# The router's steps at other places of the iteration, and exponentials first in each score unit

## What is computed

```python
h = _layernorm(x) * (1 + ca) + sa
A1 = where(causal, Q1 @ K1.T * scaling, -inf)        # per head; A2 alike
attn = softmax(A1, -1) - lam * softmax(A2, -1)
O = attn @ V;  O = O / rms(O) * rms_scale * (1 - LAMBDA_INIT)
x = x + ga * (O @ W_o.T)
h = _layernorm(x) * (1 + cb) + sb
logits = h @ router_w.T + router_b                   # 8 experts
topv, topi = top_k(logits, 2);  gates = softmax(topv)
x = x + gb * sum_e gate_e * (silu(h @ gate_w_e.T) * (h @ up_w_e.T)) @ down_w_e.T
```

## Time and profile before

| what | value |
|---|---|
| time, median of 3 runs | 1676.66 us (1676.61 to 1682.93) |
| profiled execution, device time | 1678.91 us |
| its span, first to last instruction | 1677.1 us |
| what lies around the span | 1.8 us |
| busy: PE / DVE / ACT / POOL | 1340.8 / 1228.7 / 859.4 / 857.3 us |
| mean granted TensorE clock | 0.903 of full |

### The profile page before, as it was taken

The page is one execution under the profiler, slowest core; times in us unless marked ns, Lnnn a source line. Parts: engine busy times, 40 slices in busy tenths (PEclk is TensorE's granted clock), DMA queues, the critical chain, the costliest instruction groups (busy, mean ns, idle before and its releaser), DMA issues. The chain is left out here.

```text
span 1677.1 us, 44178 instructions
## 1 busy us (share of the span) xinstructions
PE 1340.8 (80%) x14048; PEld 940.4 (56%) x14049; DVE 1228.7 (73%) x3090; ACT 859.4 (51%) x1918; POOL 857.3 (51%) x1283
## 2 busy tenths in 40 slices
PE   1578888888888888888888888885199999999960
PEld 0345555555555555555555555553178888888850
DVE  3467887888888888888888888876756666666647
ACT  1156667666766676667666766664123333333320
POOL 0135566666666666666666666665323333333334
PEclk9999989998999899989998999896589999999985
DMA  5453444344434443444344434410111111111129
GB/s 203 99 111 76 112 109 101 86 111 109 105 85 108 112 105 84 111 111 105 83 111 111 106 83 108 105 39 17 43 44 44 44 44 46 43 44 45 44 76 296
DMA packets 182624, 151.73 MB, mean 90 GB/s; under 512 B 29555, under 2 KB 165369, under 8 KB 182068
## 3 DMA queue, kind: packets, MB, share of 16 engines
q1 hardware_dynamic: 165124, 122.11, 30.2%
q0 software_dynamic: 8448, 16.93, 3.3%
q10 hardware_dynamic: 8880, 10.49, 1.8%
HBM read 88.26 MB, written 60.51 MB: 89 GB/s over the span
## 5 line engine op out<-in xcount | busy, mean ns | idle before, releaser
L1190 DVE TENSOR_REDUCE mx<-p_max 128x2 f32<-128x512 f32 (+1 forms) x768 | 504.9, 685 | 198.3 <-PE p_max L816 188.9
L1009 ACT ACTIVATE probs<-p_exp 128x512 f32<-128x512 f32 x768 | 440.4, 601 | 239.7 <-PE p_exp L837 150.9
L1430 POOL TENSOR_SCALAR_AFFINE_SELECT probs<-probs 128x256 f32<-128x256 f32 (+1 forms) x768 | 366.3, 486 | 344.6 <-ACT probs L1009 333.3
L866 PE MATMUL p_out<-probs,v 128*32 128x256 f32 (+1 forms) x4096 | 253.3, 371 | 42.1 <-ACT ot L1000 35.7
L659 POOL DMA_INDIRECT pair_out<-on,v x136 | 133.7, 983 | 282.4 <-ACT on L569 274.6
L808 PE MATMUL p_max<-kt,qt 50*128 50x256 bf16 x1024 | 199.3, 293 | 35.6 <-ACT probs L1009 19.0
L866 PEld LDWEIGHTS p_out<-probs,v 128*32 128x32 f32 x4096 | 124.0, 119 | 145.2 <-POOL probs L1430 67.9
L837 PE MATMUL p_exp<-qt,kt 52*128 52x256 bf16 x1024 | 205.2, 289 | 0.0
L816 PE MATMUL p_max<-tri,ids 64*128 64x128 bf16 (+1 forms) x768 | 188.7, 253 | 0.0
L633 DVE TENSOR_TENSOR ot<-ot,p_max 128x512 f32<-128x512 f32 x136 | 93.5, 688 | 123.6 <-PE p_max L520 105.0
L816 PE MATMUL p_max<-tri,idb 64*128 64x128 bf16 (+1 forms) x768 | 172.3, 252 | 0.0
(11 more groups left out here) (174 smaller groups left out, 2750.5 us busy)
## 6 DMA issues: line engine op xcount, KB each, us to landing
qt<-q_parts SPq DMA_DIRECT2D x128, 192.0 KB
q_parts<-part_h SPq DMA_DIRECT2D x96, 128.0 KB, 1.9
kt<-k_parts SPq DMA_DIRECT2D x128, 96.0 KB
v<-rows_sorted SPq DMA_DIRECT2D x136, 65.0 KB, 1.8
q_parts<-part_m SPq DMA_DIRECT2D x64, 128.0 KB, 1.9
kt<-k_parts SPq DMA_DIRECT2D x128, 64.0 KB
qt<-pair_out SPq DMA_DIRECT2D x32, 256.0 KB, 5.0
mods<-mod_rows SPq DMA_DIRECT2D x32, 192.0 KB
```

The costliest lines, as they stand in the source:

```text
L866: m = nc.tensor.matmul(p_out[32 * j:32 * j + 32, pair, SEQ - n:SEQ], v[:, b.par, tile, 2 * g + head, :], src, start=(tile == 0), stop=(til ...
L1009: nc.scalar.activation(probs[:, quad % 2, k, :], p_exp[:, n % 3, :], ACT.Exp, scale=SCALE).then_inc(exp_done.sem, 1)
L1190: V.reduce_max(mx[:, w, tile, t, heads[0]:heads[-1] + 1], p_max[:, bank, :].rearrange("p (h k) -> p h k", h=len(heads)), AX.X, negate=True ...
L1430: G.affine_select(out=blocks, in_=blocks, compare_op=ALU.is_ge, fill=zero, base=0, pattern=[[0, count], [1, P]], channel_multiplier=-1).th ...
```

## The change

Router steps move, and the order inside a score unit is turned round. PE: logits from s=7 to s=5; the two `outputs_to_rows` of half 1 from s=5 and 6 (banks 1 and 0) to s=5 and 7 (banks 0 and 1); ranks from s=10 to s=11. DVE: `lg` from s=8 to s=6, the top eight from s=9 to s=7, the second `normalise` of half 1 from s=7 to s=8, after `minus_max`; statistics of bW from s=8 and 9 to s=10; positions from s=11 to s=12. ACT: `gexp` from s=10 to s=9. POOL: `o` from s=8 to s=9, `osq` from s=9 to s=10, scatters from one in each of s=12 to 15 to one in s=13, two in s=14 and one in s=15. The work is the same, and so is its amount.

```diff
-        MISC0 = [(ht_ready, 1, 2), (r_ready, 1, 2), (r_ready, 2, 2), (on2_ready, 4, -1),
+        MISC0 = [(ht_ready, 1, 2), (r_ready, 1, 2), (r_ready, 2, 2), (on2_ready, 3, -1),
                  (v_ready, 1, 1), (on2_ready, 1, 0)]
         MISC1 = [(nmt_ready, 2, 0), (ont_ready, 1, -2), (attn_scaled, 1, -2), (h2t_ready, 1, -3),
-                 (on2_ready, 3, -1), (route, 1, -3), (nmt_ready, 1, 1), (route, ROUTE_CARRY, -3),
+                 (route, 1, -3), (on2_ready, 4, -1), (nmt_ready, 1, 1), (route, ROUTE_CARRY, -3),
                  (on2_ready, 2, 0)]
...
-                for _ in itertools.zip_longest(max_unit(bm, n), exp_unit(be, n)):
+                for _ in itertools.zip_longest(exp_unit(be, n), max_unit(bm, n)):
...
                     if s == 5 and active(bC):
-                        outputs_to_rows(i, bC, 1, 0, 1, 4)
-                    if s == 6 and active(bC):
-                        outputs_to_rows(i, bC, 1, 1, 0, 3)
+                        outputs_to_rows(i, bC, 1, 0, 0, 3)
...
-                    if s == 7 and active(bR):
-                        mix_free(pe, i, 1, 5)
+                    if s == 5 and active(bR):
+                        mix_free(pe, i, 1, 4)
                         wait(pe, h2t_ready, bR)
...
                         m.then_inc(lg_ps.sem, 1)
+                    if s == 7 and active(bC):
+                        outputs_to_rows(i, bC, 1, 1, 1, 5)
...
-                    if s == 10 and active(bR):
+                    if s == 11 and active(bR):
 
                         mix_free(pe, i, 1, 7)
                         wait(pe, route, bR, ROUTE_BOTH)
...
-                    if s == 10 and active(bR):
+                    if s == 9 and active(bR):
                         wait(act, route, bR, ROUTE_TOP)
...
                     if s == 6:
+                        if active(bR):
+
+                            wait(dve, route, bR.plus(-1))
+                            wait(dve, lg_ps, bR)
+                            V.tensor_tensor(lg[:], p_mix[:, 1, 0:NT * NE].rearrange("p (t e) -> p t e", t=NT),
+                                            rb[:].unsqueeze(1).to_broadcast([P, NT, NE]), ALU.add).then_inc(route.sem, 1)
                         for k in range(2):
                             if active(bC):
-                                normalise(bC, 1, 0, 1, k)
+                                normalise(bC, 1, 0, 0, k)
...
-                    if s == 7 and active(bC):
-                        for k in range(2):
-                            normalise(bC, 1, 1, 0, k)
+                    if s == 7 and active(bR):
+                        wait(dve, route, bR, 1)
+                        settle(dve)
+                        for tile in range(NT):
+                            V.max(top8[:, tile, :], lg[:, tile, :]).then_inc(route.sem, 1)
                     if s == 8:
                         if active(b1):
                             minus_max(b1, 0, 0)
                             minus_max(b1, 0, 1)
...
+                        if active(bC):
+                            for k in range(2):
+                                normalise(bC, 1, 1, 1, k)
...
+                    if s == 10 and active(bW):
+                        wait(dve, x1_ready, bW)
+                        settle(dve)
+                        statistics(bW, 1, stats2)
+                        for tile in range(NT):
+                            mean_and_variance(bW, 1, stats2, tile)
...
                     if s == 11:
                         inverse_roots(i, [0])
+                    if s == 12:
                         if active(bR):
 
                             wait(dve, rank_ps, bR)
...
-                    if s == 12:
                         hrow = h2[:, bR.par].rearrange("p j t r -> p (j t) r")
...
-                    if s == 8 and active(bC):
+                    if s == 9 and active(bC):
 
                         wait(pool, on2_ready, bC)
...
-                    if s == 9 and active(bC):
+                    if s == 10 and active(bC):
                         wait(pool, o_ready, bC)
...
-                    if s in (12, 13, 14, 15) and active(bR):
-
-                        k = s - 12
+                    for k in {13: (0,), 14: (1, 2), 15: (3,)}.get(s, ()):
+                        if not active(bR):
+                            continue
```

More of the change, by code:

```diff
@@ L1316, in body @@
                     if s == 6:
-                        for k in range(2):
-                            if active(bC):
-                                normalise(bC, 1, 0, 1, k)
-                            if active(bL):
-                                mean_and_variance(bL, 0, stats1, k)
-                    if s == 7 and active(bC):
-                        for k in range(2):
-                            normalise(bC, 1, 1, 0, k)
[L1325 to L1328, removed]
                         if active(bR):
@@ L1334, in body @@
                                             rb[:].unsqueeze(1).to_broadcast([P, NT, NE]), ALU.add).then_inc(route.sem, 1)
[L1335 to L1338, removed]
-                    if s == 9:
[L1340 to L1347, removed]
+                        for k in range(2):
+                            if active(bC):
+                                normalise(bC, 1, 0, 0, k)
+                            if active(bL):
+                                mean_and_variance(bL, 0, stats1, k)
+                    if s == 7 and active(bR):
[3 more added lines that the diff above has]
+                            V.max(top8[:, tile, :], lg[:, tile, :]).then_inc(route.sem, 1)
+                    if s == 8:
+                        if active(b1):
+                            minus_max(b1, 0, 0)
+                            minus_max(b1, 0, 1)
+                        if active(bC):
+                            for k in range(2):
+                                normalise(bC, 1, 1, 1, k)
+                    if s == 9:
                         if active(bR):
```

## The result

The changed kernel takes 1685.82 us (median of 19 runs), the one before, run alongside, 1680.43; the ratio is 1.0039, 95% interval 1.0021 to 1.0058. That is 0.4% slower: clear of noise, within the 0.5% that the prediction calls no change, and opposite to the forecast of 1618 us. Ratios leave out executions in a slower state that shows now and then, so they can differ a little from the quotient of the medians.

A forecast was written before the change was run, and what follows sets the result against it. PE bounds steps 0 to 5, DVE the rest. Per iteration 2.16+2.06-1.5-0.3=2.4 us, taken as 2.1; over 28 iterations 59 us, so 1618 us for the median; likeliest case 1604 to 1642, whole range 1602 to 1688.

The forecast's parts named there:

- its two halves: One iteration: PE bounds steps 0 to 5, busy 8.55 of 9.30 us; DVE bounds the rest, busy 19.59 of 22.20.
- light stretch of PE: From 573.4 to 579.4 us PE is busy only 3.35 of 6.00; right after it the clock stands at half for 6.8.
- the idle time of DVE that goes: DVE's waits of 0.70, 0.93 and 0.43 us for PE go if the clock stays at 2.4 GHz: 2.06, 0.5 left.
- the first term: DVE saves 2.16 us an iteration because `minus_max` no longer meets `o` and `topf` no longer meets `osq`.
- if nothing new collides: Condition on DVE's saving of 2.16 us: the moved POOL operations hold no other DVE operation.
- Rival 2: `o` meets `chosen` or `both` and DVE stands still for nearly 1.28 us; time 1668 to 1695 us; chance 0.22.
- The forecast's upper end: Slow end of the forecast's range, 1642 us, beside a smallest gain of 39 us over the loop.
- The pair of units: Exponentials first delay the second unit's maximum by 0.11 or 0.22 us; exposed at s=3 and s=5, 0.3 an iteration.
- Rival 3: The clock's fall moves to steps 0 to 4, where PE bounds; 36 us slower if in all iterations, 1713; chance 0.08.
- Moved at no cost: `gexp` on ACT, the scatters on POOL and half 1's second `normalise` in step 8 move without adding time.
- The wait for `osq`: In step 11 `rms_ss` waits for `osq`, now one step later on POOL: 0.2 us added.
- the statistics directly behind each other: On DVE the aggregations follow their own statistics directly: 0.1 us added.

## Why the prediction was wrong

**What bounds the kernel.** Right in its two halves, and in that DVE waits inside its instructions. That the DVE-bound part and the light stretch of PE are coupled was read from the rows as well, but not priced: the idle time of DVE that goes, 2.06 us less 0.5, was one term of a sum, though it hangs wholly on the other terms. Those terms came out small, and the waits it counts on are still there.

**The step that failed** is the condition under the first term, "if nothing new collides". The sum takes DVE's 2.16 us as saved; what the changed kernel shows an iteration is 1.08 at `minus_max` (1.28 forecast) and 0.68 at `topf` (0.88), less 1.03 that `both` loses to `o`: 0.73 in place of 2.16. The kernel before had one long collision in step 9, `osq` on `topf`, the changed one has another, `o` on `both`, and it adds the one on `on_tok`. Rival 2 had the mechanism, the place and the margin: `both` against `o` within 0.1 us. Counted from the take of n=13, `o` came as reckoned, 1.66 us after it against 1.64, and `both` at 1.77 against 1.54; 0.19 of those 0.23 us are `topf`, taken at 0.16 us and measured at 0.35 beside the masks. Rival 2 was given 0.22; a race that the working itself finds undecided deserved about half. Its time, 1668 to 1695, holds the result, as does its statement that PE's stretch stays light and n=16 comes no earlier. By the Trainium skill (SBUF — State Buffer, Who interferes with whom) whichever of the two operations issues first keeps the ports and the other stands; `both` at 1.20 us behind `o`, and at 0.17 once `o` runs ahead of the masks, agree with it. `on_tok` doesn't: it starts 0.29 to 0.36 us ahead of the mask and still loses, and there the measurement decides.

**The size, given the condition.** Without the collisions the changed kernel takes 1615 us against the 1618 forecast; the mean period goes down by 2.65 us from the changed kernel and by 2.18 from the one before, against 2.1. That the forecast comes out there is luck in part. The kernel with `osq` alone moved, whose `minus_max` is held as before, gets to the same time from 0.95 us at `topf` and `chosen`, worth 2.54 us an iteration, where the forecast needed every term. The forecast's upper end should by its own 39 us have been 1638, not 1642; nothing hangs on it.

**The pair of units** was priced at 0.3 us an iteration of PE; it costs none, and the order alone gains 8 us on the kernel before. The step rested on products starting in the order of issue. The Trainium skill (TensorE: Matmul & The Clock Gate, Part 3) has that order as strict; the trace of a pair disagrees, with 561.25 for the product issued second and 561.48 for the first, and the measurement decides.

**Rival 3** placed a fall of the clock in steps 0 to 4 and gave as its cause a lighter turn of the iteration. Six of 25 iterations have it, after `on_tok` was held for 2.7 us, a collision that no step of the prediction named: it looked for POOL's `o` and `osq` and not for the masks and the product of step 0. It costs 15 to 17 us. In all six a scatter of the iteration before ends right ahead of the mask; whether the moved scatters or DVE's shifted steps bring the operations together was not tested.

**Moved at no cost.** `gexp`, the logits, the second `normalise`: no wait of PE, DVE or ACT names them in the trace after. The scatters aren't named either, but see rival 3. The wait for `osq` (0.2) and the statistics directly behind each other (0.1) show only as gaps of 0.3 us at most.

## What to carry to other kernels

Where two engines exclude each other for a whole instruction, as DVE and POOL do here, a short operation pays the length of the long one beside it (0.17 us became 1.20), so read the durations of tiny operations first: 1.03 us for four elements a row was worth 63 us. Moving steps in a hand-made order moves every such meeting; each operation of the one engine wants to be laid against each of the other at its new place, and a margin of 0.1 us is a coin toss. After an edit, check in the trace that the order on the engine changed and the collision is gone: one move here changed neither. And where PE's clock falls after a light stretch, the microsecond that makes the stretch light can be worth two to three, as it was here.

## What the runs showed of the hardware

Products on opposite halves of the array's rows start out of the order of issue (0.23 us early in a pair). POOL's in-place mask, with one input, also holds DVE operations: `chosen` 0.34 us beside masks and 0.19 alone, `topf` 0.35 and 0.23, and the mask beside `on_tok` is held by it in turn (1.11 us for 0.64). A DVE operation can lose its turn several times in a row, 0.68 us becoming 2.75, though it started 0.33 us ahead of the first of them. And the clock falls without any long pause of PE: in the light stretch of the kernel before its longest wait is 1.12 us, and it was busy 3.35 of 6.00 us.
